# A decoder layer with a mixture of experts: tokens routed beside the attention, two batches at a time, into one DRAM region per expert

## The reference, cut to what matters

```python
x = _layernorm(x + attn(x, qkv_w, qkv_b, out_w, out_b))
x = _layernorm(x + xattn(x, ctx, ctx, WQ, bQ, WK, bK, WV, bV, WO, bO, lens))
logits = x @ router_w                          # 1600 tokens x 14 experts
assignments = argmax(logits)                   # first of equals
weights = softmax(logits)[assignments]
hid = gelu(x @ w1[e] + b1[e])                  # 256 -> 512, exact gelu
x = _layernorm(x + weights * (hid @ w2[e] + b2[e]))
```

## Time and profile before

| | us |
|---|---|
| median of 3 runs | 585.12 (585.09 to 586.41) |
| the profiled execution, its own time | 585.6 |
| its span, first to last instruction | 583.8 |
| PE, DVE, ACT, POOL busy | 496.3, 358.8, 328.3, 246.4 |
| mean granted TensorE clock | 0.933 |
| DMA moved | 37.83 MB |

### The profile page before, as it was taken

How to read it: one execution, slowest core, us unless ns; L and a number is a source line. 1 busy time by engine, 2 the same in 40 slices (tenths; PEclk the granted TensorE clock), 3 DMA queues, 4 the chain that set the end, 5 groups by cost and what they waited for, 6 DMA issues and landing times. The chain is left out here.

```text
span 583.8 us, 13740 instructions
## 1 busy us (share of the span) xinstructions
PE 496.3 (85%) x4777; PEld 424.1 (73%) x4778; DVE 358.8 (61%) x942; ACT 328.3 (56%) x1468; POOL 246.4 (42%) x338
## 2 busy tenths in 40 slices
PE   0567999999999999999999999999986139889760
PEld 0356688987988888788798878879876128789650
DVE  1597867768667667866866786684353832344441
ACT  2367687766768666686766668676461003243331
POOL 2176634424334443442543344343040443666664
PEclk9996999999999999999999999999988558899895
DMA  7760000000000000000000000000000839898321
GB/s 177 160 159 1 16 10 23 9 16 15 16 8 10 22 8 16 23 9 8 8 25 8 9 15 10 8 1 9 9 2 14 274 114 341 285 296 278 102 46 30
DMA packets 40483, 37.83 MB, mean 65 GB/s; under 512 B 18118, under 2 KB 34060, under 8 KB 40292
## 3 DMA queue, kind: packets, MB, share of 16 engines
q1 hardware_dynamic: 38212, 32.19, 18.4%
q0 software_dynamic: 2208, 4.83, 2.9%
HBM read 33.73 MB, written 4.00 MB: 65 GB/s over the span
## 5 line engine op out<-in xcount | busy, mean ns | idle before, releaser
L677 POOL TENSOR_TENSOR probs<-probs,row_inv 100x400 f32<-100x400 f32 x128 | 116.7, 933 | 158.9 <-DVE row_inv L871 158.9
L734 ACT ACTIVATE probs<-bank,neg_max 100x100 f32<-100x100 f32 x512 | 171.8, 387 | 20.8 <-DVE neg_max L866 20.0
L734 ACT ACTIVATION_READ_ACCUMULATOR probs<-bank,neg_max 100x1 f32 x512 | 127.1, 248 | 0.0
L866 DVE TENSOR_REDUCE neg_max<-bank 100x4 f32<-100x400 f32 x128 | 68.4, 564 | 12.9 <-PE bank L1042 6.6
L1073 PE MATMUL bank<-ident,probs 100*100 100x100 f32 x512 | 68.0, 256 | 3.1 <-POOL probs L677 2.1
L1073 PEld LDWEIGHTS bank<-ident,probs 100*100 100x100 f32 x512 | 49.3, 130 | 12.8 <-POOL probs L677 4.6
L878 DVE COPY probsT<-bank 100x400 f32<-100x400 f32 x76 | 43.1, 567 | 14.7 <-PE bank L1073 14.5
L743 ACT COPY probsT<-bank 100x400 f32<-100x400 f32 x52 | 27.2, 523 | 28.7 <-PE bank L1073 28.7
L681 POOL TENSOR_TENSOR rstd<-var_eps,half_power 100x1 f32<-100x1 f32 x32 | 17.9, 561 | 58.2 <-DVE var_eps L917 58.2
L1358 ACT ACTIVATE hT<-bank,b1c 128x128 f32<-128x128 f32 x72 | 20.7, 376 | 32.4 <-PE bank L1324 25.1
L950 PE MATMUL bank<-WO_h,oX_h 128*100 128x256 f32 x128 | 38.2, 298 | 0.0
(11 more groups left out here) (195 smaller groups left out, 1319.1 us busy)
## 6 DMA issues: line engine op xcount, KB each, us to landing
w1s<-in_L_ffn_w_dram SPq DMA_DIRECT2D x18, 512.0 KB
w2s<-in_L_ffn_w_dram SPq DMA_DIRECT2D x18, 512.0 KB
b2r<-in_L_ffn_b_dram SPq DMA_DIRECT2D x1, 1792.0 KB, 12.4
xs<-in_x_dram SPq DMA_DIRECT2D x16, 100.0 KB
cs<-in_ctx_dram SPq DMA_DIRECT2D x16, 100.0 KB
token_rows<-y SPq DMA_DIRECT2D x16, 100.0 KB
qX<-in_L_xattn_WK_dram SPq DMA_DIRECT2D x2, 512.0 KB, 4.7
qX<-in_L_xattn_WV_dram SPq DMA_DIRECT2D x2, 512.0 KB, 4.5
```

The source lines that it names most:

```text
L677: probs_ready.mark(pool.tensor_tensor(v, v, r, ALU.mult), step)
L734: i = act.activation(probs[:, k % SLOTS, w], sc_bank[p % 2 * 2 + u][0:T, w], ACT.Exp, bias=neg_max[:, k % SLOTS, h:h + 1], accum_out=row_s ...
L866: max_ready.mark(dve.tensor_reduce(neg_max[:, k % SLOTS, :], src, AX_X, ALU.max, negate=True), step)
```

## The change

Routing moves into `PLAN`. After each pair of batches' logits: `top.n` and `choose.n` (DVE: top logit, first expert with it, one-hot `chosen`), `count.n` (DVE: running one-hot sum `so_far`), `gate.n` (ACT: exp of the shifted logits with its sum), `rank.n` (PE: two bf16 matmuls into a projection bank), `place.n` (DVE: gate, and the row number expert x 1664 + rank), `id.n` (POOL: the token's number beside its row) and `scatter.n` (POOL: an indirect DMA of 100 rows of 258 words into `expert_rows`). `y2` has six buffers instead of four, and the steps' order in `STEPS` is new in most lines after the first four. `store.n` is gone.

`expert_rows` has 15 regions of 13 x 128 rows. It is filled beforehand with empty rows: a DMA of SP per 128 rows of every region, DRAM to DRAM, behind each of `c_load.0` to `c_load.12`.

Weights of the attention lie in tensors whose place is reused: the experts' first six pairs of weights and b2 are loaded over them as soon as the last `out`, `K`, `V` and `Q` steps are done.

The blocks' part is written out without a loop: 14 first blocks and two more always, further ones in pairs if used. A block loads plain rows of its region. The gate and the output index come with the row. All 14 experts' weights have a buffer of their own; blocks 14 and on share two. The order of the block's steps on PE is as before.

```diff
+CAP = P * (MORE + 1)
+ROW = D + 2
+Y2S = 6
+OB = 2
...
-PROJECTIONS = ("xT", "qk", "v", "qkT", "cT", "K", "out", "yT", "V", "Q", "wo", "rT", "logits")
+PROJECTIONS = ("xT", "qk", "v", "qkT", "cT", "K", "out", "yT", "V", "Q", "wo", "rT", "logits", "rank")
...
-    rows = nc.dram_tensor("token_rows", [B * T, D], F32, kind="Internal").ap()
+    rows = nc.dram_tensor("expert_rows", [(NE + 1) * CAP, ROW], F32, kind="Internal").ap()
...
+                for dst, src in ((before[:, :], c_before), (less[:, :], c_less), (token_id[:, :], c_token)):
+                    sp.dma_start(dst, src).then_inc(route_in, 16)
+
+                def empty(j):
+                    chunk = rows.rearrange("(e j r) w -> e j (r w)", e=NE + 1, r=P)[:, j, :]
+                    sp.dma_start(chunk, c_empty.rearrange("(o r) w -> o (r w)", o=1).broadcast_to([NE + 1, P * ROW])).then_inc(emptied[j // 2], 16)
+
...
                         with sp.Else():
                             sp.dma_start(cs[:, n % 2, :], ctx[n, 0:T, :]).then_inc(c_in[n % 2], 16)
-                    elif kind == "store":
-                        wait(*ln_done.at(("ln", "x", n)))
-                        sp.dma_start(rows[n * T:(n + 1) * T, :], y2[:, n % YS, :]).then_inc(y_stored[n % YS], 16)
+                        if n < CAP // P:
+                            empty(n)
...
+                for last, first in ((("out", B - 1), 0), (("K", NG - 1, UB - 1), 2), (("V", B - 1, 1), 4)):
+                    wait(*projected.at(last))
+                    for k in (first, first + 1):
+                        sp.dma_start(held_w1[k][:, :, :], w1[k].rearrange("(c p) f -> p c f", p=P)).then_inc(w_in[k], 16)
+                        sp.dma_start(held_w2[k][:, :, :], w2[k].rearrange("(c p) d -> p c d", p=P)).then_inc(w_in[k], 16)
+                wait(*projected.at(("Q", NG - 1, UB - 1)))
+                sp.dma_start(b2r[:, :, :], b2.rearrange("(o e) d -> o e d", o=1).broadcast_to([P, NE, D])).then_inc(b2_in, 16)
...
+                    elif kind == "scatter":
+
+                        for j in range(((n + 1) * T - 1) // P // 2 + 1):
+                            wait(emptied[j], 16 * min(2, CAP // P - 2 * j))
+                        wait(*id_ready.at(("id", n)))
+                        wait(*taken(("rank", n // GB)))
+                        wait(*ln_done.at(("ln", "x", n)))
+                        pool.indirect_dma_start(out=rows, out_offset=bass.IndirectOffsetOnAxis(ap=place_i[:, n:n + 1], axis=0),
+                                                in_=y2[:, n % Y2S, :], in_offset=None).then_inc(scattered[n % Y2S], 16)
...
+                    elif kind == "top":
+
+                        two = slice(GB * n, GB * (n + 1))
+                        wait(*took.at(("logits_out", GB * n)))
+                        wait(*took.at(("logits_out", GB * n + 1)))
+                        dve.tensor_reduce(top_logit[:, two], logits_all[:, two, :], AX_X, ALU.max).then_inc(top_ready, 1)
+                        top_found.mark(dve.tensor_reduce(neg_top[:, two], logits_all[:, two, :], AX_X, ALU.max, negate=True), step)
...
+                    elif kind == "rank":
+
+
+                        at = 2 * (n % 2)
+                        wait(route_set, 3)
+                        wait(*counted.at(("count", n)))
+                        pe.matmul(ps[0:T, 0:GB * NE], before_b[:, :], chosen[:, :, :].rearrange("p j e -> p (j e)"), start=True, stop=False)
+                        i = pe.matmul(ps[0:T, 0:GB * NE], ones_b[:, 0:T], so_far[:, at:at + 2, :].rearrange("p j e -> p (j e)"), start=False, stop=True)
...
     @block.sync
     def _(sp):
...
+        for k in range(Y2S):
+            sp.wait_ge(scattered[k], 16 * len(range(k, B, Y2S)))
+        for (a, b), s in zip(X_LOADS, x_loaded):
+            sp.dma_start(xin[:, a:b, :], rows.rearrange("(e j r) w -> r e j w", e=NE + 1, r=P)[:, a:b, 0, :]).then_inc(s, 16)
+        for n in range(EARLY_WEIGHTS, NE):
+            sp.dma_start(w1s[n][:, :, :], w1[n].rearrange("(c p) f -> p c f", p=P)).then_inc(w_in[n], 16)
+            sp.dma_start(w2s[n][:, :, :], w2[n].rearrange("(c p) d -> p c d", p=P)).then_inc(w_in[n], 16)
...
+        def load_more(n):
+            k, i = (n - NE) % OB, n - NE
+            e = sp.value_load(expert_i[0:1, i:i + 1], min_val=0, max_val=NE - 1)
+            at = sp.value_load(home_i[0:1, i:i + 1], min_val=0, max_val=(NE + 1) * (CAP // P) - 1)
+            if n >= ALWAYS:
+
+                sp.wait_ge(res_ready, n - OB + 1)
+                sp.wait_ge(out_stored[(n - OB) % SLOTS_R], 16 * ((n - OB) // SLOTS_R + 1))
+            sp.dma_start(x_more[k][:, :], blocks_of_rows[bass.ds(at, 1)].rearrange("o r w -> r (o w)")).then_inc(x_more_in[k], 16)
...
+        def run(blocks):
+            for n in blocks:
+                x, s, count = x_of(n)
+                pool.wait_ge(ve_ready, n + 1)
+                pool.tensor_tensor(rs[:, n % 2, :], ve[:, n % 2, :], half_power[:, :], ALU.pow).then_inc(rs_ready, 1)
+                pool.wait_ge(s, count)
+                pool.wait_ge(res_ready, n + 1)
+                pool.indirect_dma_start(out=flat, out_offset=bass.IndirectOffsetOnAxis(ap=x[:, D + 1:ROW].bitcast(I32), axis=0),
+                                        in_=res[n % SLOTS_R][:, :], in_offset=None, bounds_check=B * T - 1, oob_is_err=False).then_inc(out_stored[n % SLOTS_R], 16)
```

More of the change, by code:

```diff
@@ new lines @@
+Q_out.1.1 wo.1 copy_v.s.4.0.1 pv.s.4.0 added.x.1 qkT.5 o_hi.s.4.0 stats.x.1 id.1 turn.s.4.1.0 qkT_out.5 K.1.3
+copy_a.s.4.1.0 o_lo.s.4.0 rstd.x.1 keys_v.5 ln.x.1 turn.s.4.1.1 K_out.1.3 rT.1 copy_v.s.4.1.1 scores.s.5.0 rT_out.1
+logits.1 max.s.5.0.0 pv.s.4.1 max.s.5.0.1 exp.s.5.0.0 V.2.0 logits_out.1 max.s.5.1.0 top.0 o_hi.s.4.1 max.s.5.1.1
+exp.s.5.0.1 Q.1.2 o_lo.s.4.1 choose.0 count.0 gate.0 scores.x.2.0 V_out.2.0 Q_out.1.2 inv.s.5.0 norm.s.5.0.0
+exp.s.5.1.0 rank.0 max.x.2.0.0 out.4 norm.s.5.0.1 place.0 exp.s.5.1.1 turn.s.5.0.0 added.s.4 Q.1.3 scatter.0
@@ new lines @@
+norm.s.6.1.0 o_hi.x.3.1 Q.2.1 copy_v.s.6.0.0 norm.s.6.1.1 o_lo.x.3.1 turn.s.6.0.1 Q_out.2.1 wo.3 copy_v.s.6.0.1
+pv.s.6.0 added.x.3 qkT.7 o_hi.s.6.0 stats.x.3 id.3 turn.s.6.1.0 qkT_out.7 K.2.3 copy_a.s.6.1.0 o_lo.s.6.0 rstd.x.3
+keys_v.7 ln.x.3 turn.s.6.1.1 K_out.2.3 rT.3 copy_v.s.6.1.1 scores.s.7.0 rT_out.3 logits.3 max.s.7.0.0 pv.s.6.1
+max.s.7.0.1 exp.s.7.0.0 V.4.0 logits_out.3 max.s.7.1.0 top.1 o_hi.s.6.1 max.s.7.1.1 exp.s.7.0.1 Q.2.2 o_lo.s.6.1
+choose.1 count.1 gate.1 scores.x.4.0 V_out.4.0 Q_out.2.2 inv.s.7.0 norm.s.7.0.0 exp.s.7.1.0 rank.1 max.x.4.0.0 out.6
@@ new lines @@
+norm.s.8.1.1 o_lo.x.5.1 turn.s.8.0.1 Q_out.3.1 wo.5 copy_v.s.8.0.1 pv.s.8.0 added.x.5 qkT.9 o_hi.s.8.0 stats.x.5
+id.5 turn.s.8.1.0 qkT_out.9 K.3.3 copy_a.s.8.1.0 o_lo.s.8.0 rstd.x.5 keys_v.9 ln.x.5 turn.s.8.1.1 K_out.3.3 rT.5
+copy_v.s.8.1.1 scores.s.9.0 rT_out.5 logits.5 max.s.9.0.0 pv.s.8.1 max.s.9.0.1 exp.s.9.0.0 V.6.0 logits_out.5
+max.s.9.1.0 top.2 o_hi.s.8.1 max.s.9.1.1 exp.s.9.0.1 Q.3.2 o_lo.s.8.1 choose.2 count.2 gate.2 scores.x.6.0 V_out.6.0
+Q_out.3.2 inv.s.9.0 norm.s.9.0.0 exp.s.9.1.0 rank.2 max.x.6.0.0 out.8 norm.s.9.0.1 place.2 exp.s.9.1.1 turn.s.9.0.0
@@ new lines @@
+copy_v.s.14.0.1 pv.s.14.0 added.x.11 qkT.15 o_hi.s.14.0 stats.x.11 id.11 turn.s.14.1.0 qkT_out.15 K.6.3
+copy_a.s.14.1.0 o_lo.s.14.0 rstd.x.11 keys_v.15 ln.x.11 turn.s.14.1.1 K_out.6.3 rT.11 copy_v.s.14.1.1 scores.s.15.0
+rT_out.11 logits.11 max.s.15.0.0 pv.s.14.1 max.s.15.0.1 exp.s.15.0.0 V.12.0 logits_out.11 max.s.15.1.0 top.5
+o_hi.s.14.1 max.s.15.1.1 exp.s.15.0.1 Q.6.2 o_lo.s.14.1 choose.5 count.5 gate.5 scores.x.12.0 V_out.12.0 Q_out.6.2
+inv.s.15.0 norm.s.15.0.0 exp.s.15.1.0 rank.5 max.x.12.0.0 out.14 norm.s.15.0.1 place.5 exp.s.15.1.1 turn.s.15.0.0
@@ L239 @@
+scatter.15
 """
@@ L256, in taker @@
         return (kind + "_lo",) + step[1:]
+    if kind == "rank":
+        return ("place",) + step[1:]
     if kind in ("out", "wo"):
@@ L978, in do @@
                             wait(*ln_done.at(("ln", "x", n)))
[L979 removed]
+                            src = y2[:, n % Y2S, 0:D]
                         for c in range(KC):
@@ L1423, in _ @@
+        run(list(range(ALWAYS)))
+        pool.wait_ge(more_ready, 3)
+        for first in LATER:
+            with pool.If(in_use(pool, first)):
+                run(list(range(first, first + OB)))
     @block.vector
```

980 lines of the change are left out of this document (477 added, 503 removed).

## The result

| | before | after |
|---|---|---|
| median of 4 runs each, us | 585.76 (585.09 to 586.48) | 609.49 (607.71 to 612.92) |
| profiled execution, its own time | 585.6 | 610.39 |
| span | 583.8 | 608.4 |
| mean granted TensorE clock | 0.933 | 0.922 |

The change makes the kernel slower: ratio 1.0402, 95% interval 1.0375 to 1.0428. The predicted 587.6 was 22 us too low, and the time lies above the range of 570 to 604.

A forecast was written before the change was run, and what follows sets the result against it. The middle of the attention was taken as bound by PE. The terms +21.3 + 4 − 16.3 − 1.7 − 4.7 = +2.6 on 585.6 gave 588.1, as a median 587.6 us; range 570 to 604.

The forecast's parts named there:

- the price of the routing in the attention: Attention: routing pieces in every pair of batches, mostly hidden, 0.5 us a pair and the matmuls, +4 us.
- Rival 2: Middle of the attention suffers, DVE and POOL serving in order: 2 us a pair, 599.6 us; chance 0.16 with rival 4.
- rival 4: Block stage stays at POOL's old round or rows come late: adds 12, 600 us; chance counted with rival 2.
- The sign given for it: Middle of the attention: PE waiting for POOL's `probs` or DVE's copies would make the +4 us wrong.
- the term's own upper bound of +26: Attention: the scatters' 3.8 us of seven pairs all on the path, instead of +4 us.
- The start: Up to the first exp: four fills of 6.0 us each ahead of weight pieces delay it by +21.3 us.
- Rival 1: Start hardly delayed, loads overtaking or sharing with the fills: +5 there, 571.3 us; chance 0.26.
- rival 3: Fills: DRAM to DRAM copies run at half rate, adding 19.2, 606.8 us; chance 0.10.
- The nine later fills: Fills after the start, where DMA is 5% busy: cost nothing, covered by the context loads' lead.
- From logits to fc1: Last logits to the first block: first fc1 at +11.8 instead of 28.15 us, −16.3 us.
- The blocks: Block stage: 61.1 us, then a wait ahead of blocks 16 and 17; together 81.9 instead of 83.65, −1.7 us.
- The tail: After the last fc2: 14.6 us instead of 19.3, −4.7 us.

The follow-up runs named there:

- two_early: The changed kernel with two fills at the start, behind the loads of ctx 0 and 1, and the other eleven late: 592.8 us.
- late_fills: The changed kernel with its 13 fills issued later, behind the last weight piece and loads of x: 586.9 us, ratio 0.9999 to the kernel before.
- old_order: The changed kernel with attention steps in the order of the kernel before, all routing behind the last logits, no scatters of batches 0 to 11: 602.6 us.

## Why the prediction was wrong, point by point

**What failed: the price of the routing in the attention.** The step said "I take 0.5 us a pair and the matmuls, **+4 us**". It measured 27.4 for the stage. The mechanism had been named just ahead of it: `scatter` waits on POOL for `place`, "and queued behind it are a `norm` and a `rstd`, for which PE's `turn` and DVE's `ln` wait". Then it was priced by busy shares ("With 72% of the time used on DVE and 41% on POOL most is hidden"). A share says how much work fits, not whether an instruction stands ahead of one that PE needs next. The order was written out in `STEPS`, with `scatter.0 ... scatter.1 ... rstd.s.4` on POOL, and could have been followed. The runs put 4.65 us a pair together as follows: new order 0.95, routing work on DVE, ACT and PE 0.41, scatters as such 0.54, and their place ahead of the rstd 2.76. Six pairs give 27.9, and the stage's 27.4 are 0.5 less, at the edges. These are differences of single executions; the last is the least firm, since the clock fell in four of the six pairs here and in two of six in two_early, whose attention has the same steps and a pace of 53.91. The 0.5 us a pair was meant for all four; the routing work alone used it up.

**The rival was right in kind.** Rival 2 had the middle suffer at 2 us a pair, 599.6, with 0.16 together with rival 4. The kind is shown, the size was 4.65. The sign given for it was not quite the one that came: it named waits for POOL's `probs` or DVE's copies, and PE waited for DVE's `y` behind POOL's `rstd`. Its evidence against ("its waits are short and POOL idles 59%") is the same slip. And the range stopped short: the term's own upper bound of +26 gives 587.6 + 22 = 609.6, and the range ended at 604, against its own bound. That 609.6 is also the time that came is luck: the bound had seven pairs with 3.8 us of scatters each on the path, where six pairs lost 4.65 to four causes, and the tail came out 4.4 us better than its term.

**What the trace of before showed in part.** That `y` stands still beside POOL was there to be read, 0.81 us against 0.41 in five pairs; that it would run 1.33 us longer beside two multiplications, and with PE waiting, was not. Nor was it that PE's clock would fall in the middle: the lower clock stood in the earlier trace rows beside a long idle stretch (0.50 from 452.7 on), and PE's longest wait from 60 to 400 us was 0.6 us. These made a hold of 1.7 us into 2.76.

**The start: right.** +22.8 against +21.3; WQ_h cast at 55.75 against "near 57". The price of a fill came out at 5.7 us against the kernel before, by four fills and by two, and at 4.7 to 5.2 against late_fills, where 6.0 was taken. Rival 1 is refuted by both runs, and rival 3: at half rate the first exp would have come 19 us later. There was more to it than the reason given: loads did not only wait behind the fills, SP took 10.86 and 6.11 us to issue two of them.

**The nine later fills: right, nothing.** In the run with the late fills all thirteen lie behind the start, and no cost shows; old_order has nine in the middle at the pace of the kernel before.

**From logits to fc1: right.** 12.3 against 11.8. **The blocks: right in sum, with two errors.** The first 16 took 60.5 us (61.1 predicted). The hole and blocks 16 and 17 took 22.5 (20.8 predicted): the output of block 15 landed after 5.48 instead of 2.36 us beside the weights of block 16. The hole was foreseen; that it could be had back for two more buffers was not looked at. Two figures were a little off on the way: "3.78 against 2.10" is 1.7 us, not 1.85 (which is nearer to 3.78 against an undisturbed 1.95), and in the attention's step a pair is "some 46" us, where it was 49.98. Neither moves the sum by much.

**The tail: right in sign, half in size.** 10.2 against 14.6. To the landing of the last output it is 8.0 us, as worked out (8.1). But 1.6 was put in for a table load and the mark, and the trace after has no table load there (why was not tried), and 4.9 from the mark to the end, where 2.05 are left.

## What to carry to other kernels

In a kernel whose main engine never waits, price a moved instruction by its place: write down, for each in-order engine, what stands behind it and who waits for that, and treat the helper's idle share as no cover. Bulk copies with no deadline go behind the last load that has one, above all in a stage whose DMA engines are full. Where buffers are used again only for the last few blocks, look at what the reuse waits for: here two buffers more gave back 15.3 us, about what the shorter handover had gained. And before two engines are released by the same event, look whether either runs longer beside the other: one more wait was worth 12 us here.
